# RWKV attention and a Hadamard FFN in fp32 halves: eight products per inner tile and pair of chunks against seven, and the gate by Silu

## The reference

```python
shifted = xn one token earlier, zero at a row's start
xk, xv, xr = (mu * xn + (1 - mu) * shifted for three mu vectors)
r, k, v = xr @ Wr.T, xk @ Wk.T, xv @ Wv.T
wkv = the stabilised RWKV-v4 recurrence over tokens (running maximum, numerator, denominator)
att = (sigmoid(r) * wkv) @ Wo.T
hidden = fwht(silu(xn @ W1.T) * (xn @ W3.T))        # 2048 wide, Walsh-Hadamard
out = x + att + hidden @ W2.T
```

## Time and profile before

| what | value |
|---|---|
| median of three runs | 2851.76 us (2851.28 to 2851.79) |
| the profiled execution's own time | 2851.35 us |
| its span, first to last instruction | 2849.5 us |
| TensorE, DVE, ACT busy | 2823.4, 2014.9, 921.1 us |
| moved by DMA | 546 MB, 192 GB/s |

### The profile page before, as it was taken

One profiled execution on the slowest core, in us unless ns is written; L12 is line 12 of the kernel. 1 busy time (PEld: TensorE's weight loads), 2 busy tenths in 40 slices (PEclk: granted clock), 3 DMA queues, 4 the chain that ended last, 5 costly groups with the idle time before them and its releaser, 6 DMA issues.

```text
span 2849.5 us, 36275 instructions
## 1 busy us (share of the span) xinstructions
PE 2823.4 (99%) x12352; PEld 2318.1 (81%) x12352; DVE 2014.9 (71%) x2888; ACT 921.1 (32%) x1571; POOL 97.8 (3%) x70
## 2 busy tenths in 40 slices
PE   7999999999999999999999999999999999999999
PEld 4778888888888888888888888888888888888887
DVE  5796767767677775767757677676776767767575
ACT  5444242242322324223242332423224242242321
POOL 0450000000000000000000000000000000000000
PEclk9999999999999999999999999999999999999999
DMA  9777555455555655546455555554545555464554
GB/s 349 248 253 273 185 170 200 163 201 178 185 184 169 207 170 187 193 165 205 162 200 183 174 194 169 191 184 170 200 168 198 178 185 187 165 212 167 172 171 148
DMA packets 168930, 545.97 MB, mean 192 GB/s; under 512 B 20416, under 2 KB 20544, under 8 KB 166464
## 3 DMA queue, kind: packets, MB, share of 16 engines
q1 hardware_dynamic: 168896, 545.53, 56.4%
HBM read 492.97 MB, written 52.49 MB: 191 GB/s over the span
## 4 chain that ended last, share of the span: by engine, by line
PE 96%; DVE 2%; DMA 1%; ACT 0%; issue 0%; POOL 0%; SPq 0%; ACTq 0%; DVEq 0%
PE bank L481 16%; PE bank L483 16%; PE bank L482 16%; PE acc L498 10%; PE acc L497 10%; PE acc L496 10%; PE bank L458 6%; PE bank L457 6%; PE bank L459 6%; PE acc L542 1%; PE acc L519 0%; DMA raw<-units_w 0%; DMA raw<-units_r 0%; DMA fly<-units_w 0%; DVE pab L773 0%; DMA xrow<-x 0%
## 5 line engine op out<-in xcount | busy, mean ns | idle before, releaser
L481 PE MATMUL bank<-xs,ring 128*128 128x512 f32 x1564 | 609.3, 390 | 2.5 <-POOL ring L420 2.4
L483 PE MATMUL bank<-xs,ring 128*128 128x512 f32 x1564 | 608.5, 389 | 0.0
L482 PE MATMUL bank<-xs,ring 128*128 128x512 f32 x1564 | 608.5, 389 | 0.0
L496 PE MATMUL acc<-ring,hid 128*128 128x512 f32 x1024 | 398.4, 389 | 0.4 <-POOL ring L420 0.4
L498 PE MATMUL acc<-ring,hid 128*128 128x512 f32 x1024 | 398.8, 389 | 0.0
L497 PE MATMUL acc<-ring,hid 128*128 128x512 f32 x1024 | 398.3, 389 | 0.0
L859 DVE SCALAR_TENSOR_TENSOR hidf<-hidf,bank 128x512 f32<-128x512 f32 x256 | 175.6, 686 | 284.0 <-ACT hidf L630 284.0
L641 ACT ACTIVATE hid<-hidf 128x512 fp32r<-128x512 f32 x256 | 162.1, 633 | 659.3 <-DVE hidf L862 659.3
L481 PEld LDWEIGHTS bank<-xs,ring 128*128 128x128 f32 x1564 | 293.6, 188 | 65.6 <-DVE hidf L862 3.0
L483 PEld LDWEIGHTS bank<-xs,ring 128*128 128x128 f32 x1564 | 293.6, 188 | 61.0
L482 PEld LDWEIGHTS bank<-xs,ring 128*128 128x128 f32 x1564 | 293.5, 188 | 61.1 <-issue 0.2
(11 more groups left out here) (94 smaller groups left out, 4046.9 us busy)
## 6 DMA issues: line engine op xcount, KB each, us to landing
ring<-split_units SPq DMA_DIRECT2D x780, 512.0 KB, 3.3
split_units<-ring SPq DMA_DIRECT2D x60, 512.0 KB, 4.1
xt<-x_t SPq DMA_DIRECT2D x16, 1024.0 KB, 7.9
res<-x SPq DMA_DIRECT2D x16, 1024.0 KB, 6.4
xrow<-x SPq DMA_DIRECT2D x15, 1024.0 KB, 5.3
out<-res SPq DMA_DIRECT2D x15, 1024.0 KB, 6.0
mix<-token_rows SPq DMA_DIRECT2D x16, 512.0 KB, 4.2
raw<-units_w SPq DMA_DIRECT2D x32, 256.0 KB, 4.6
```

What stands on the lines that cost most here:

```text
L481: pe.matmul(banks[b + n][:, :], w[:, 0, col], xs[:, 0, kt, :], start=kt == 0, stop=False)
L482: pe.matmul(banks[b + n][:, :], w[:, 1, col], xs[:, 0, kt, :], start=False, stop=False)
L483: last = pe.matmul(banks[b + n][:, :], w[:, 0, col], xs[:, 1, kt, :], start=False, stop=kt == KT - 1)
L496: pe.matmul(acc[tt][:, :], a[:, 0, col], w[:, 0, :], start=first, stop=False)
```

## The change

Two neighbouring chunks A and B (1024 tokens) are now one pair; there are 8 pairs. For inner tile j the two weight tiles (W1, W3), the near and far half of the 512 channels and the two chunks form a 2 by 2 by 2 block product, and it is computed with seven block products (Winograd's form of Strassen's scheme) of six matmuls each, in the order 1, 2, 6, 5, 7, 3, 4. Sums of the weight tiles are made once in pair 0 by POOL (`make_sums`), sums of the activations once per pair by DVE (`right_made`, four operations of 1024, and `right_lo`, seven of 1024), high parts by ACT (`right_hi`, seven of 1024). Partial sums stay in PSUM (three banks `gamma`, one `alpha`) and are copied out by ACT where a later product goes on adding to the same bank:

```diff
+            def product(s, j, piece):
+                i, half_unit = LEFT_AT[piece]
+                bank = alpha if piece == 2 else gamma[(j + 2) % 3] if piece in (5, 3) else gamma[j % 3]
+                fresh = piece in (1, 2, 5)
...
+                if piece == 1:
...
+                        wait(pe, gate_b_sum, s, j - 1)
+                elif piece == 2:
...
+                        wait(pe, gate_a_sum, s, j)
+                elif piece == 5:
...
+                        wait(pe, ha_full, s, j)
+                else:
+                    wait(pe, u_copied, s, 4 * j + {6: 1, 7: 2, 3: 3, 4: 4}[piece])
+                for kt in range(2):
...
```

Conditions for the first and last tile and pair are left out below. TensorE's order, per inner tile (`down_a` adds to the accumulators of chunk A, one tile of three matmuls at a time; tile 0 has none) and per pair. The hidden tiles of chunk B are stored to DRAM (`spilled`) and used after the up stage, one unit in turn with one of the next pair's r, k, v units:

```diff
+            def up_step(s, j):
+                product(s, j, 1)
+                product(s, j, 2)
+                down_a(s, i, (0,))
+                product(s, j, 6)
+                product(s, j, 5)
+                down_a(s, i, (1,))
+                product(s, j, 7)
+                product(s, j, 3)
+                down_a(s, i, (2,))
+                product(s, j, 4)
+                down_a(s, i, (3,))
+                if j in EXTRA_AT:                      # 5, 8, 10
+                    down_a(s, EXTRA_AT[j], range(TT))
+            def pair(s):
+                for j in range(FT):
+                    up_step(s, j)
+                down_a(s, ND - 2, range(TT))
+                r_unit(s + 1, 0)                       # not in the last pair, nor those below
+                down_a(s, ND - 1, range(TT))
+                for n in range(1, 4):
+                    r_unit(s + 1, n)
+                for i in range(ND):                    # 20
+                    down_b(s, i)
+                    r_unit(s + 1, 4 + i)
```

The gate goes from tanh on ACT and a multiplication by (tanh + 1) on DVE to one ACT operation; DVE adds the partial sums:

```diff
-                    act.activation(f[:, :], banks[2 * (j % 2)][:, :], ACT.Tanh, scale=0.5)
-                    g = step(dve.scalar_tensor_tensor(f[:, :], f[:, :], 1.0, banks[b][:, :], ALU.add, ALU.mult))
+                act.activation(fb, u_two[j % 2], ACT.Silu).then_inc(gate_b, 1)
+                act.activation(fa[j % 2], p_one[j % 2], ACT.Silu).then_inc(gate_a, 1)
```

The recurrence has 8 stages per item. Item 0 of a pair stands in the down stage before it (n = 10 to 17), items 1 to 6 in the up stage (three stages per inner tile), item 7 in its own down stage (n = 0 to 7). The four exponentials come from two differences, as exp(-relu(z)) and exp(-relu(-z)), in operations of 1024:

```diff
+            def rectified(r, w):
+                wait(act, exp_arg, r, 2 * w + 2)
+                act.activation(e_one[:, :, :], z[:, :, :], ACT.Relu)
+                act.activation(e_two[:, :, :], z[:, :, :], ACT.Relu, scale=-1.0)
+            def exponentials(r, w):
+                for i, of in enumerate((e_one, e_two)):
+                    act.activation(of[:, :, :], of[:, :, :], ACT.Exp, scale=-1.0)
```

ACT's order per inner tile (starts is 0 for j = 3, 11; 1 or 2 for j = 0, 5, 8, 13; None for the others) and per step n of the down stage:

```diff
+            def up_step(s, j):
+                copy_sum(s, j, 1, p_one[j % 2])
+                gate_b_silu(s, j - 1)
+                if starts == 0:
+                    rectified(s, w)
+                copy_sum(s, j, 6, u_two[j % 2])
+                copy_sum(s, j, 5, p_five)
+                hidden_a_hi(s, DOWN_A.index(("w2", j - 1)))
+                if starts == 0:
+                    exponentials(s, w)
+                copy_sum(s, j, 7, u_three)
+                gate_a_silu(s, j)
+                if starts is not None and starts > 0:
+                    rectified(s, w)
+                    exponentials(s, w)
+            def down_step(s, n):
+                if n % KT == KT - 1:
+                    evacuate(r, n // KT)
+                mix_second(r, n + MIX_AHEAD)           # waits for r_unit n
+                mix_first(r, n + MIX_AHEAD + 1)
+                if 2 <= n < 2 + ND:
+                    hidden_b_hi(s, n - 2)
+                if n == 1:
+                    rectified(s, 7)
+                    exponentials(s, 7)
+                if n == 11:
+                    rectified(r, 0)
+                    exponentials(r, 0)
+                if 13 <= n < 20:
+                    right_hi(r, n - 13)
```

DVE's, in which `wkv` stage 1 makes the arguments of the exponentials:

```diff
+            def up_step(s, j):
+                hidden_a(s, j - 1)
+                recurrence(s, j, 0)
+                gate_a_added(s, j)
+                hidden_b(s, j - 1)
+                recurrence(s, j, 1)
+                hidden_a_lo(s, DOWN_A.index(("w2", j - 1)))
+                recurrence(s, j, 2)
+                normalisation(s + 1, j)
+                b_added(s, j)                          # two additions
+            def down_step(s, n):
+                mix_item(r, n + MIX_AHEAD + 1)
+                mix_rest(r, n + MIX_AHEAD)
+                if n in (2, 3):
+                    add_residual(s, 0, range(2 * n - 4, 2 * n - 2))
+                if 2 <= n < 2 + ND:
+                    hidden_b_lo(s, n - 2)
+                if n < 4:
+                    centre(r, 1, n // 2) if n % 2 == 0 else scale(r, 1, n // 2)
+                if n < 8:
+                    wkv(s, 7, n)
+                if 10 <= n < 18:
+                    wkv(r, 0, n - 10)
+                if 13 <= n < 17:
+                    right_made(r, n - 13)
+                if n >= 17:
+                    right_lo(r, n - 17)
```

More of the change, by code:

```diff
@@ L75, in in_slot @@
[L75 to L92 removed]
+SCRATCH = 1024
+PIECES = (1, 2, 6, 5, 7, 3, 4)
@@ new lines, in down_b @@
+            def down_b(s, i):
+                wait(pe, hb_hi, s, i + 1)
+                wait(pe, hb_lo, s, i + 1)
+                w = down_b_weights(s, i)
+                for tt in range(TT):
+                    if i == 0:
+                        wait(pe, out_ready, s, tt + 1)
+                    last = down_tile(w, hid[(i + ND) % SLOTS], tt, i == 0, i == ND - 1)
+                    if tt == TT - 1:
+                        last.then_inc(db_done, 1)
+                    elif i == ND - 1:
+                        last.then_inc(acc_b_tile, 1)
@@ L504, in ffn_down @@
[L504 to L512 removed]
+                        last.then_inc(r_bank_done, 1)
             def turn_across_tiles():
@@ L730, in mix_item, with wide, token_stats @@
-            def mix_item(t, n):
-                q, kt = divmod(n, KT)
+            def wide(a):
+                return a.broadcast_to([P, 2, N])
+            def token_stats(r, h, q):
+                first = isinstance(r, int) and r == 0
+                if first:
+                    dve.wait_ge(x0_loaded[2 * h + q], 16)
+                else:
+                    wait(dve, x_loaded, r - 1, 16 * (2 * h + q + 1))
+                for t in range(2):
+                    dve.bn_stats(stats[:, 4 * h + 2 * q + t, :],
+                                 x0[:, 4 * h + 2 * q + t, :] if first else xrow[:, t, :]).then_inc(stats_made, 1)
```

1663 lines of the change are left out of this document (1038 added, 625 removed).

## The result

| what | value |
|---|---|
| changed kernel, median of four runs | 2958.44 us (2953.58 to 2960.76) |
| kernel before beside it, median of four | 2851.52 us (2848.70 to 2851.79) |
| ratio, with its 95% interval | 1.0375 (1.0357 to 1.0393) |
| profiled execution's own time | 2956.52 us |

The changed kernel is slower, as forecast, but by 107 us where 10 were forecast, and the time lies 23 us above the upper end of the range. The sum was made for one profiled execution; against this one's 2956.5 it misses 95.5 us.

What follows compares the result with a forecast made beforehand. TensorE was taken as the bound: 174 us of matmuls saved against added costs of 40 + 84 + 6 + 11 + 14 + 7 + 22 = 184, so +10 on 2851.35, 2861 us; range 2775 to 2935 (own mechanism 2825 to 2890).

Steps and rivals of the forecast that it cites:

- What bounds the kernel, and what is removed: Whole run: TensorE sets the time at 0.2267 us per matmul; 768 fewer up-stage matmuls save 174.1 us.
- The up stage: Inner tiles 0, 3 and 11: ACT's table switches make TensorE wait, 5.0 us per pair, +40 over 8 pairs.
- the rival of a longer switch: ACT's table switch takes 2.6 us instead of 1.37: 60 us more in all, 2921 us; chance 0.17.
- The down start: Before down_b(0): a 15.6 us line through ACT and DVE holds TensorE; 12.0 us in each of seven pairs, +84.
- Its second piece: Down start, third tile: TensorE waits 1.9 us more for the third residual tile, behind centre, mix_item and mix_rest.
- the 1.6 forecast at n = 11 (+11): Down stage, n = 11 and 12: next pair's first recurrence item delays hidden_b_lo(10), 1.6 us by seven pairs, +11.
- The rest of a middle pair: Middle pair, cut from the prediction afterwards: 326.4 us of steps plus waits of 5.0, 12.0, 1.6 and 2.0, 347.0 us.
- Start ... Together +22: Start and first pair: delays by x, exponentials, stores and DVE, plus POOL's splits in pair 0; +22 us (5 to 45).
- the term "(+3)" for chunk B's x ahead of W2: Start: 1 MB more of x goes ahead of W2, delaying the first r unit by 3 us.
- +10: First pair: POOL's splits and sums take about 11 of 12.24 us per tile, ACT has 2.8 more; +10 us.
- The sign: Whole kernel: slower by 0.3%, +10 us; chances slower 0.52, same 0.13, faster 0.35.
- The transfers: DMA loads in the down stage: +14 us over seven pairs, and +7 for down weights in the last pair.

Runs made afterwards that it cites:

- the experiment on ACT's order: Against the changed kernel, ACT's rectified(s, 7) and exponentials(s, 7) moved from down-stage step n = 1 to n = 3, behind hidden_b_hi(1); 2901.47 us.

## Why the prediction was wrong, and where it was right

**What bounds the kernel, and what is removed: right but for pair 0.** 768 matmuls went, and an eighth product put back costs 158 us. In pair 0 it costs nothing, so 21.8 of the 174.1 us were counted as saved in a pair that others pace. (The forecast count of 11,552 in all should have been 11,584: I had not taken both passes of the turning, 64 matmuls.)

**The up stage: right.** Tile 1 waits 2.2 in the middle pairs, forecast 2.6; tiles 3 and 11 together 1.9, forecast 2.4; tiles 5, 8 and 13 pass. In pair 2 the waits on ACT's copies are 4.1 together, forecast 5.0. The price of a switch, 1.37 against 1.40, and the number of loads, 105 to 115 against 113, held, and the rival of a longer switch fell. Without switches 35.8 of the 40.9 us of these waits are gone.

**The down start: right in place, line and size** for the seven pairs (9.75 against 10.1), and the experiment on ACT's order takes two thirds of it away. Its second piece, 1.9 on the third residual tile, isn't there: no wait on `res` stands in the list of TensorE's waits of pair 2. I had let that tile need it 1.36 us after the first matmul; at half clock they need 2.7. Nor is there a wait like the 1.6 forecast at n = 11 (+11): apart from the starts of the down stages the waits on the hidden tile come to about 1 us in the whole run.

**The rest of a middle pair: too low by 3.8.** By the view of windows TensorE is busy 333.3 us in one of the six, on average, and waits 17.5, against 20.6 (in pair 2: 10.5 on the hidden tile, 9.8 of it at the down start; 4.1 on ACT's copies; 1.6 at the first matmul of the next pair's up stage, which had no term, and which the view puts down to ACT's `kvr` at two pairs and to nothing at three; 0.9 on DMA). But 1440 steps are only 326.4. The prediction priced every matmul at 0.2267; it had no term for the time around a wait: the matmul ahead of it ends 0.16 later than its step, the first ones behind it take 0.34 to 0.58 to the next, and some six to eight more take 0.43. So the waits were priced 3.1 too high and the pace 6.9 too low.

**"Start ... Together +22" is the step that failed**, by 25 + 44 = 69 us.
- At the start, the term "(+3)" for chunk B's x ahead of W2 was worked out as a delay of transfers. It was a wait on DVE's in-order queue, 11.4 us, for the store of rows that nobody needed yet, and ACT's copies of W2's first pass stand behind it in the chain. The run that moves this wait gave 10.4, not all of it in the start.
- "exponentials go ahead of the copies of the turn (+2)" measured 5.7 (TensorE's wait on ACT's copies of the second pass), and a reversal of that order, with one load moved, gave 8.4. The other two terms held: 2.5 at r_unit 14 for the "(+3)", and 4.7 at r_unit 20, on ACT behind a late DVE, for the "(+4)".
- The rest of the start's 25 us had no term: some 7 us by which the matmuls ran further behind their steps than in the start of the kernel before, at a mean granted clock of 0.93 instead of 1.00. Which of the start's waits bring that on is open.
- In pair 0, "about 11 of 12.24 us per tile with the sums" for POOL was right (181.5 us for 16 tiles, 11.3 each), and "+10" was the wrong price for it. The error: DVE's durations were taken from the earlier trace rows, means over a run in which POOL is busy 3% of the time, and put into a stage in which POOL works 181.5 of 401.3 us. Operations with two inputs in SBUF take 0.94 to 1.15 there, not 0.69. I had said that DVE has 9.6 of 12.24 us to do; with POOL busy it has 12.4, and that margin is gone. TensorE's waits in pair 0 come to 52.7 us where 30.6 was forecast, and its busy time to 348.4 where 1440 steps are 326.4: these two make up the 44. With POOL's work narrowed, pair 0 came to 358.4.

**The sign was right, half by luck.** In the steady state the reason given holds: waits and pace cost 24.4 us in a middle pair, where 96 steps fewer save 21.8, and 350.8 us stand against 348.2 for two old chunks. My forecast had 347.0, so a small gain there, and took its loss from the start; most of the measured loss is in the start and pair 0.

**The transfers** were not the bound: 26.6 us on `vring` in the whole run, forecast 14 + 7; 13.5 in the first seven pairs and 13.1 in the last.

## What to carry to other kernels

When a change lengthens a stage in which another engine is busy, take durations from a stage with the same neighbours, not from a mean over the run: here a DVE operation cost 1.15 us beside POOL and 0.69 without it, and the pair in which it did gained nothing from matmuls saved. When work on the bottleneck is cut, list for each in-order queue what stands ahead of the operation that it waits for next; one block moved two places down ACT's queue was worth 57 us, a third of what the new scheme had saved. Spend as much care on the first pair as on the steady state: 69 of 96 us of this miss lay there.

## What the runs showed of the hardware

- While POOL runs its own tensor operations, DVE's operations with both inputs in SBUF slow down, from 688 to 1152, from 676 to 1127 and from 686 to 936 ns in the mean, and one with an input in PSUM doesn't (676 in both). The Trainium skill, "GPSIMD Engine Reference" (Specifications), says that the two engines share their SBUF interfaces and get in each other's way where DVE has two SBUF inputs; this trace agrees, and the run with POOL's work narrowed (689) as well.
- A change of ACT's table costs 1.40 us here: 1.31 between neighbouring operations, which overlap by 0.09 to 0.10 without it. Ahead of the 112 loads between Silu and Exp ACT idles 2.0 us in all (1.0 + 0.6 + 0.4 in the rows above), so none of them has a drain ahead of it.
- Behind waits of 2.2 us the granted clock fell in some pairs to the lower of its two levels for seven or eight matmuls (0.43 us from one to the next), and in others not; the pairs took the same time. Behind the wait of 9.75 us in pair 2, and behind one of 3.2 in the run with the exponentials later, the six after the first started 0.43 us apart. The mean granted clock fell from 1.000 to 0.974.
